# Tail values as 16 blocks in both attentions of a two-layer cross-attention kernel; other fillers, seeds, additions and mask conversions

## What is computed

```python
x = x + tanh(g_xattn[0]) * L0_xattn(layernorm(x), ctx_1024)            # no mask
x = x + tanh(g_ffn[0])   * L0_ffn(layernorm(x))                        # 512 -> 2048 relu -> 512
x = x + tanh(g_xattn[1]) * L1_xattn(ctx_1024, layernorm(x), mask)      # q, k, v normalised, masked
x = x + tanh(g_ffn[1])   * L1_ffn(layernorm(x))                        # fixed-point gelu
# attention: scores = q.k / sqrt(32); softmax over 154 keys; probs @ v; heads joined; @ W + b
```

## Time and profile before

| | |
|---|---|
| median of 3 executions | 2407.02 us (2404.2 to 2410.87) |
| the profiled execution | 2409.38 us, its span 2407.6 us |
| mean granted TensorE clock | 0.991 |
| VectorE, ScalarE, GpSimd busy | 1504.9, 1181.1, 238.6 us |
| memory traffic | read 105.30 MB, written 33.55 MB |

### The profile page before, as it was taken

One profiled execution on the slowest core, in us unless ns is written; L12 is line 12 of the kernel. 1 busy time (PEld: TensorE's weight loads), 2 busy tenths in 40 slices (PEclk: granted clock), 3 DMA queues, 4 the chain that ended last, 5 costly groups with the idle time before them and its releaser, 6 DMA issues.

```text
span 2407.6 us, 32695 instructions
## 1 busy us (share of the span) xinstructions
PE 2352.2 (98%) x12984; PEld 1793.4 (74%) x12984; DVE 1504.9 (63%) x2467; ACT 1181.1 (49%) x1912; POOL 238.6 (10%) x219
## 2 busy tenths in 40 slices
PE   7999999999999999999988999999999999999998
PEld 5566666688888888888765666666788888888886
DVE  5566666442222222223488888886988987988986
ACT  4554434442222222223335666666666666666665
POOL 1021112210000000000111111113000000000000
PEclk9999999999999999999998999999999999999999
DMA  3121112421101101102311111224301001110000
GB/s 130 36 88 53 53 54 80 161 80 53 50 4 53 53 1 53 53 3 86 121 64 50 67 68 67 67 71 145 105 29 43 36 36 36 36 38 33 36 35 19
DMA packets 89159, 140.95 MB, mean 59 GB/s; under 512 B 5040, under 2 KB 27952, under 8 KB 89008
## 3 DMA queue, kind: packets, MB, share of 16 engines
q1 hardware_dynamic: 89008, 138.87, 16.9%
HBM read 105.30 MB, written 33.55 MB: 58 GB/s over the span
## 4 chain that ended last, share of the span: by engine, by line
PE 39%; DVE 8%; ACT 2%; issue 2%; POOL 0%; DVEq 0%; ACTq 0%
PE l_lay_bank L69 19%; PE l_lay_score L69 11%; PE l_lay_score L1490 1%; PE l_lay_score L1546 1%; PE l_lay_score L1563 1%; DVE l_at_at_next L1089 1%; PE l_lay_score L1575 1%; PE l_lay_score L1567 1%; DVE l_at_h_lo L1103 1%; DVE l_at_at_next L1082 1%; PE l_lay_bank L1406 1%; DVE l_at_full L1078 1%; DVE l_at_full L1071 1%; DVE l_at_xTf_lo L975 1%; DVE l_at_maxes L1012 1%
## 5 line engine op out<-in xcount | busy, mean ns | idle before, releaser
L69 PE MATMUL l_lay_score<-l_at_tw_hi,l_at_h_hi 128*128 128x512 f32 x1024 | 401.5, 392 | 5.4 <-DVE l_at_h_lo L1103 4.8
L69 PE MATMUL l_lay_bank<-l_at_xTf_hi,l_at_tw_hi 128*128 128x512 f32 x1024 | 400.0, 391 | 0.0
L69 PE MATMUL l_lay_score<-l_at_tw_hi,l_at_h_lo 128*128 128x512 f32 x1024 | 398.8, 389 | 0.0
L69 PE MATMUL l_lay_bank<-l_at_xTf_hi,l_at_tw_lo 128*128 128x512 f32 x1024 | 398.4, 389 | 0.0
L69 PE MATMUL l_lay_bank<-l_at_xTf_lo,l_at_tw_hi 128*128 128x512 f32 x1024 | 398.4, 389 | 0.0
L69 PE MATMUL l_lay_score<-l_at_tw_lo,l_at_h_hi 128*128 128x512 f32 x1024 | 398.4, 389 | 0.0
L1063 DVE TENSOR_TENSOR l_at_h_lo<-l_at_full,l_at_h_hi 128x512 fp32r<-128x512 f32 x128 | 93.4, 729 | 468.5 <-ACT l_at_h_hi L760 468.5
L755 ACT ACTIVATE l_at_full<-l_lay_bank,l_at_lay_b 128x512 f32<-128x512 f32 x128 | 88.5, 691 | 456.6 <-PE l_lay_bank L69 456.6
L69 PEld LDWEIGHTS l_lay_score<-l_at_tw_hi,l_at_h_hi 128*128 128x128 f32 x1024 | 192.2, 188 | 49.3 <-DVE l_at_h_lo L1103 10.4
L69 PEld LDWEIGHTS l_lay_score<-l_at_tw_hi,l_at_h_lo 128*128 128x128 f32 x1024 | 192.2, 188 | 40.3
L69 PEld LDWEIGHTS l_lay_bank<-l_at_xTf_hi,l_at_tw_hi 128*128 128x128 f32 x1024 | 192.3, 188 | 40.1 <-issue 0.7
(11 more groups left out here) (196 smaller groups left out, 4063.0 us busy)
## 6 DMA issues: line engine op xcount, KB each, us to landing
both_x_in<-stream SPq DMA_DIRECT2D x25, 1024.0 KB, 5.6
l_at_xg<-stream SPq DMA_DIRECT2D x23, 1024.0 KB, 5.5
stream<-l_at_xg SPq DMA_DIRECT2D x22, 1024.0 KB, 4.3
l_at_tw_raw<-in_l_w SPq DMA_DIRECT2D x64, 256.0 KB, 5.5
both_x_in<-in_x SPq DMA_DIRECT2D x9, 1024.0 KB, 7.8
l_at_xg<-in_x SPq DMA_DIRECT2D x7, 1024.0 KB, 5.5
out<-l_at_xg SPq DMA_DIRECT2D x7, 1024.0 KB, 4.3
l_at_maskT_in<-in_maskT SPq DMA_DIRECT2D x16, 256.0 KB, 3.5
```

The source lines that it names most:

```text
L69: done = nc.tensor.matmul(out, lhs[a], rhs[b], start=first and n == 0, stop=last and n == len(passes) - 1)
```

## The change

Tail values of all four groups are made at once, in `tail_values` on TensorE: sixteen 32x32 blocks, group 0 into `values`, groups 1 to 3 into the score banks 1 to 3, where the tail scores have been read. VectorE copies group 1's to `c_sb`, ScalarE those of groups 2 and 3 (`tail_values_out`). The main values then start an accumulation of their own except in group 0. ScalarE's `c_evict` remains for group 0 only; for groups 1 to 3 VectorE adds the bank to `c_sb` (`c_add`), and `c_out` counts that. `tail_values` comes after the first q quarter (plain) or its first half (masked).

Plain layer: a q quarter stands between scores t-1 and t for every t, instead of two between values 0 and scores 2; two of the low parts and one `c_add` go between the first maxima.

Masked layer: q quarters 0 and 1 are cut in halves around `tail_values` and scores 0; each of the first two reciprocal transposes goes ahead of scores 1 and values 0; seeds are two by VectorE and two by ScalarE for each group; `mask_front` goes between VectorE's first two seeds, `maskT_front` to before the seeds of group 1, `norm_apply` to before q row 3. The output projection waits for low parts one by one.

```diff
@@ -701,9 +702,12 @@
                 act.wait_ge(maskT_done, 2 * it + 2)
-                act.wait_ge(exp_done, NS * it + GH * t + GH)
-                nc.scalar.activation(score[:, GH - 1, :], mask_main[:, it % 2, :], ACT.Copy)\
-                    .then_inc(act_seeded, 1)
+                for j in (2, 3):
+                    act.wait_ge(exp_done, NS * it + GH * t + j + 1)
+                    if t == 0:
+                        act.wait_ge(tail_v_act, 2 * it + j - 1)
+                    nc.scalar.activation(score[:, j, :], mask_main[:, it % 2, :], ACT.Copy)\
+                        .then_inc(act_seeded, 1)
 
@@ -719,6 +723,12 @@
                         .then_inc(exp_done, 1)
+
+            def tail_values_out(it, t):
+                act.wait_ge(tail_v_ps, 3 * it + t)
+                if it >= 2:
+                    act.wait_ge(cT_lo, KT * (it - 2) + t + 1)
+                nc.scalar.activation(c_sb[:, it % 2, t, :], score[:, t, :], ACT.Copy).then_inc(tail_v_act, 1)
 
@@ -821,33 +831,37 @@
                 exps_tail(it)
-                if norm:
-                    seed_main(it, 0)
                 if it < B:
                     v_tail_of(it)
-                if not norm:
+                if norm:
+                    tail_values_out(it, 2)
+                    tail_values_out(it, 3)
+                    seed_main(it, 0)
+                else:
                     if more:
...
                         relu_hi(0)
-                exps_main(it, 0)
-                if norm:
-                    seed_main(it, 1)
-                if not norm:
+                    tail_values_out(it, 2)
+                    tail_values_out(it, 3)
                     if more:
...
                         relu_hi(1)
+                exps_main(it, 0)
+                if norm:
+                    seed_main(it, 1)
+                if more and not norm:
+                    q_front(it + 1, (2,))
                 exps_main(it, 1)
...
                 c_evict(it, 0)
+                exps_main(it, 2)
                 if more and not norm:
-                    q_front(it + 1, (2, 3))
-                exps_main(it, 2)
+                    q_front(it + 1, (3,))
                 if norm:
                     seed_main(it, 3)
-                c_evict(it, 1)
                 if it and norm:
@@ -855,14 +869,12 @@
                     front.round_hi(act, "wd")
-                c_evict(it, 2)
                 if more and norm:
...
                     q_front(it + 1, (1,))
-                c_evict(it, 3)
                 if more and norm:
@@ -957,15 +969,20 @@
                     if it >= 2 and i:
-                        dve.wait_ge(act_seeded, KT * (it - 1))
-                        dve.wait_ge(dve_seeded, 3 * KT * (it - 1))
+                        dve.wait_ge(act_seeded, 2 * KT * (it - 1))
+                        dve.wait_ge(dve_seeded, 2 * KT * (it - 1))
                     nc.vector.tensor_scalar(to, maskT_in[:, i, :], 0, -BIG, ALU.is_equal,
...
                 dve.wait_ge(maskT_done, 2 * it + 2)
-                for j in range(GH - 1):
+                for j in range(2):
                     dve.wait_ge(exp_done, NS * it + GH * t + j + 1)
+                    if t == 0 and j == 1:
+                        if it < last:
+                            mask_front(it + 1)
+                        tail_values_out(it, 1)
+                        dve.wait_ge(tail_v_dve, it + 1)
                     nc.vector.tensor_copy(score[:, j, :], mask_main[:, it % 2, :]).then_inc(dve_seeded, 1)
@@ -1011,10 +1028,26 @@
 
+            def tail_values_out(it, t):
+                dve.wait_ge(tail_v_ps, 3 * it + t)
+                if it >= 2:
+                    dve.wait_ge(cT_lo, KT * (it - 2) + t + 1)
+                nc.vector.tensor_copy(c_sb[:, it % 2, t, :], score[:, t, :]).then_inc(tail_v_dve, 1)
+
+            def c_add(it, t):
+                c = c_sb[:, it % 2, t, :]
+                if t == 1:
+                    dve.wait_ge(tail_v_dve, it + 1)
+                else:
+                    dve.wait_ge(tail_v_act, 2 * it + t - 1)
+                dve.wait_ge(c_ps, KT * it + t + 1)
+                nc.vector.tensor_tensor(c, values, c, ALU.add).then_inc(c_out, 1)
+
             def c_back(it, ts):
...
                     c = c_sb[:, it % 2, t, :]
+                    dve.wait_ge(c_out, u + 1)
                     dve.wait_ge(rT_ps, u + 1)
@@ -1233,38 +1267,48 @@
                     q_rows_front(it + 1, (0,))
+                    maskT_front(it + 1)
                     seed_main(it, 1)
                     q_rows_front(it + 1, (1,))
-                    mask_front(it + 1)
-                    maskT_front(it + 1)
                     if it:
...
                     norm_stats(it + 2)
-                    q_rows_front(it + 1, (2, 3))
+                    q_rows_front(it + 1, (2,))
+                    norm_apply(it + 2)
+                    q_rows_front(it + 1, (3,))
                     q_norm_stats(it + 1)
                     seed_main(it, 3)
+                    c_add(it, 1)
                     q_norm_apply(it + 1)
                 else:
+                    tail_values_out(it, 1)
                     q_low(it + 1, (0, 1))
                     norm_stats(it + 2)
-                    q_low(it + 1, (2, 3))
+                    q_low(it + 1, (2,))
                     norm_apply(it + 2)
+                    q_low(it + 1, (3,))
+                    c_add(it, 1)
                 if it and norm:
...
                 elif it:
-                    c_back(it - 1, (0, 1))
-                if norm:
-                    norm_apply(it + 2)
+                    c_mult(it - 1, (0, 1))
+                c_add(it, 2)
                 if it and norm:
...
                 elif it:
-                    c_back(it - 1, (2, 3))
+                    c_mult(it - 1, (2, 3))
+                    c_low(it - 1, (0, 1))
                 if norm:
+                    c_add(it, 3)
                     q_low(it + 1, (0, 1))
...
                     max_of(it + 1, m)
+                    if m < 2 and it and not norm:
+                        c_low(it - 1, (m + 2,))
+                    if m == 2 and not norm:
+                        c_add(it, 3)
                     if m in (6, 9) and norm:
@@ -1537,18 +1590,39 @@
                         if i == 0:
-                            if not norm:
+                            if not norm and t == 0 and j == 1:
+                                pe.wait_ge(tail_v_dve, it + 1)
+                            elif not norm and t == 0 and j > 1:
+                                pe.wait_ge(tail_v_act, 2 * it + j - 1)
+                            elif not norm:
                                 pe.wait_ge(exp_done, NS * it + GH * t + j + 1)
-                            elif j < GH - 1:
-                                pe.wait_ge(dve_seeded, 3 * (KT * it + t) + j + 1)
                             else:
-                                pe.wait_ge(act_seeded, KT * it + t + 1)
+                                pe.wait_ge(dve_seeded if j < 2 else act_seeded,
+                                           2 * (KT * it + t) + j % 2 + 1)
                         nc.tensor.matmul(score[:, j, :], k2[a][rows[j], b, t, 0:P], q2[c][rows[j], t, :],
...
 
+            def tail_values(it):
+                b = it // CPB
+                pe.wait_ge(exp_done, NS * it + KT)
+                if it:
+                    pe.wait_ge(c_out, KT * it)
+                else:
+                    pe.wait_ge(kv_bias, 8)
+                if it % CPB == 0:
+                    pe.wait_ge(v_placed, V_COPIES * (b + 1))
+                for t in range(KT):
+                    for j in range(GH):
+                        c = own_rows[group_of(t, j)]
+                        to = score[own_rows[j], t, :] if t else values[own_rows[j], :]
+                        done = nc.tensor.matmul(to, keys.v_tail[c, b, t, own_rows[j]], p_tail[c, t, :],
+                                                start=True, stop=t > 0, skip_group_check=True)
+                    if t:
+                        done.then_inc(tail_v_ps, 1)
+
             def values_of(it, t):
@@ -1556,17 +1630,11 @@
                     pe.wait_ge(kv_bias, 8)
-                if t == 0 and it % CPB == 0:
-                    pe.wait_ge(v_placed, V_COPIES * (b + 1))
-                for j in range(GH):
-                    own = slice(DH * j, DH * (j + 1))
-                    nc.tensor.matmul(values[own, :], keys.v_tail[:, b, t, own], p_tail[:, t, :],
-                                     start=True, stop=False, skip_group_check=True)
                 for j in range(GH):
...
                                             keys.v_main[:, b, DH * head:DH * (head + 1)],
-                                            p_main[:, t % 2, j, :], start=False, stop=True,
+                                            p_main[:, t % 2, j, :], start=t > 0, stop=True,
                                             skip_group_check=True)
@@ -1613,8 +1681,10 @@
```

(31 more changed lines are left out.)

24 lines of the change are left out of this document (18 added, 6 removed).

## The result

| | before | after |
|---|---|---|
| median of 6 executions of each | 2406.88 us | 2422.33 us (2420.97 to 2431.23) |
| ratio, after to before | | 1.0071, 95% interval 1.0057 to 1.0084 |
| the profiled execution, its span | 2409.38, 2407.6 us | 2430.67, 2428.9 us |
| mean granted TensorE clock | 0.991 | 0.986 |

The change makes the kernel 15.4 us slower.

What follows compares the result with a forecast made beforehand. TensorE was taken to set the pace, with VectorE and ScalarE only just ahead of it. Plain layer -4.7 and masked layer +18.8 sum to +14.1 us on a median of 2407.02: forecast 2421, range 2392 to 2431.

Steps and rivals of the forecast that it cites:

- the collision: Masked chunks 2, 3, 4, 6: key-mask conversions meet GpSimd's residual addition, +2.6 waiting and +1.6 half clock, 4.9 us with common cost.
- Rival B: Waits on max 2 and scores 1 mostly absent, TensorE's saving reaches the end: 2372 in full, 2390 for half; chance 0.20.
- TensorE's saving: Tail values as one block of 1.07 us instead of 3.52, with 0.22 for shape changes: net 2.2 us per chunk.
- Rival D: The tail blocks do not run side by side: +2.4 us per chunk, partly inside waits, 2440; chance 0.03.
- Plain chunks 1 to 6: Plain layer: late maxima give back 1.4 of 2.2 us, leaving -0.8 per chunk, -4.7 for six.
- Chunk 0: Plain layer's first chunk, its maximum stage bound by VectorE: a gain of only 0.7 us.
- Plain chunk 7: Last plain chunk: no filler between scores 0 and scores 1, a wait of some 2.4 us, net +0.7.
- rival C: Every wait over 1 us also halves the clock, in masked waits and both last chunks: up to +8, 2430; chance 0.07.
- A common masked chunk: Masked layer: waits at scores 1 (+1.15), scores 3 (+0.35) and up to max 2 (+0.55) outweigh the saving: +0.7 us per chunk.
- The norm: Masked layer: applying the norm ahead of q row 3 moves 1.8 us of work and costs nothing, else under 1 us a chunk.
- Rival A: The meeting of conversions and residual addition is missed, four masked chunks fall from 4.9 to 0.7 us: 2404; chance 0.25.
- Masked chunk 7: Last chunk of the masked layer, without fillers: +0.9 us.

Runs made afterwards that it cites:

- e8: Changed kernel with residual addition later, three seeds by VectorE, new VectorE orders in both layers, last chunks' second product as filler again: 2389.52 us, 0.9920 of before.
- e1: Changed kernel, but in the masked layer GpSimd widens all four reciprocals before adding the bias to the residual: 2413.06 us, ratio to before 1.0017.
- e2: Changed kernel with the key-mask conversions put back behind q row 1, residual addition left in place: 2412.11 us, ratio to before 1.0018.
- e6: Changed plain layer with the old masked layer, VectorE's low parts spread between maxima and group 3's addition after maximum 6: 2406.35 us, ratio to before 0.9987.
- e7: Changed kernel, residual addition later except in the last chunk, VectorE's additions and low parts reordered in the masked layer: 2405.56 us, ratio to before 0.9983.
- e9: The changed kernel itself run once more, giving the second trace (profiled execution 2424.66 us): median 2421.76 us, ratio to before 1.0052.
- e3: Changed kernel, residual addition later except in the last chunk, seeds three by VectorE and one by ScalarE: 2406.23 us, ratio to before 0.9992.
- e4: Plain layer of the changed kernel with the masked layer of the kernel before: 2407.85 us, ratio to before 0.9997.
- e10: As e3, but the norm of x is applied at its old place, ahead of the low parts of groups 2 and 3: 2412.79 us, ratio to before 1.0018.
- e5: Masked layer of the changed kernel with the plain layer of the kernel before: 2433.53 us, ratio to before 1.0104.

## Why the prediction was right, and where not

The median is 2422 where 2421 was said, and the largest term, the collision, is what the runs show. That the total is right to about one us is luck. In the second trace, which is 15.3 us above that of before, the masked layer costs 14.4 where 18.8 was said, mainly because three chunks met and not four, and the plain layer with the turn costs 0.9 where a gain of 4.7 was said. The two errors cancel. (The range, too, starts at 2392, while the half case of B, which it is said to take in, is 2390.) In the order of the prediction:

**TensorE's saving.** The block takes 1.07 us, to the hundredth what the tail scores' rows gave. Rival D is out. Whether the net of 2.2 us a chunk is right could be read directly only where nothing is late, and no run has that; chunk 7 below gives an estimate of 2.4. The best case seen, e8, has plain chunks of 49.77 us, with 0.6 us of lateness still in them, against 51.02 before.

**Plain chunks 1 to 6.** The mechanism and its place were right: 0.51 us at max 2 (0.5 said), then steps longer than the usual 1.09 and 0.98 by 0.21, 0.43, 0.23 and 0.10 (0.2, 0.33, 0.33 said). Three steps late were priced and four were: -0.6 in four chunks instead of -0.8, while the first of the six gained 0.2 and the last nothing. Chunk 0 gained 1.5 where 0.7 was said. Chunks 0 to 6 gave 3.9 us, 5.4 were expected.

**Plain chunk 7.** The step that failed. I priced a wait of 2.4, set it against the saving and wrote +0.7. Up to the output projection (414.60 to 446.67 against 418.41 to 447.61) it cost 2.9. The wait itself was priced well: scores 1 stand still for 1.12 us, and then their first four matmuls start one by one behind the exponentials, 1.38 us up to the next four instead of 0.33, together 2.2. What was put at nothing is what comes behind it. The wait brought the clock down, which the forecast kept for rival C alone: from the second four of scores 1 to the last eight of the sums TensorE needs 4.44 us (430.28 to 434.72), where the kernel before needs 2.52 without its tail values, 1.9 more. Scores 3 take 0.4 more, and values 3 come 0.7 late behind the addition of group 2, which is behind two products and two low parts here too. These sum to 5.3, and 5.3 - 2.9 leaves 2.4 for the saving. TensorE's groups (scores 1, values 0), and the granted clock of 429 to 434, which is 0.66:

```profile
428.90 2.13 PE L1602 MATMUL l_lay_score<-l_at_qT_hi,l_at_k_hi 32*128 32x512 f32 x4 [1.12 <-ACT l_at_p_main L724]
...
432.25 1.79 PE L1635 MATMUL l_lay_score<-l_at_p_main,l_at_v_main 128*32 128x512 f32 x8
```

```profile
429.00:434.00 5.00, 5.00 (x28) 2.09 (x32) 1.59 (x1) 3.23 (x7) 5.00 (x2) 0.66 0.02 3
```

The remaining 1.4 us lie in the turn between the layers (from the last reciprocals to the second layer's start 776.4 before, 777.8 after). The traces with the new plain layer come in two kinds: after, e1, e2, e6, e7 and e9 have 48.4 us up to the last reciprocals and then 777.8 to 778.0, while e3, e4 and e10 have 49.96 and then 775.2. Chunk 7 and the turn together take 825.2 to 826.4 in all nine, and 822.0 in both traces with the old plain layer, so the change costs 3 to 4 us there in either kind. What makes the two kinds stays open.

**A common masked chunk.** +0.7 was said; 55.66 - 54.8 = +0.9 in e1. Scores 1 wait, spread over their first four matmuls, with ScalarE's seeds of 1.14 us behind its exponentials. In chunk 2 of the first trace they take 2.38 us to the transposes behind them, where scores 0 take 1.13, so they wait 1.25:

```profile
1373.30 1.75 PE L1602 MATMUL l_lay_score<-l_at_qT_hi,l_at_k_hi 32*128 32x512 f32 x4
...
1375.68 0.65 PE L1677 MATMUL l_lay_bank<-ident,l_at_r_wide 128*128 128x128 f32 x4
```

The prediction said 1.15; its own terms, 4.42 - 3.2, give 1.2, as 4.4 - 3.99 give 0.4 for scores 3 and not 0.35 (0.38 in the trace, 1.51 against 1.13). From the q transposes to max 2 it is 6.54 us in e1 (1439.48 to 1446.02) against 6.0 before, +0.54 against +0.55 said. Within it lie two waits, values 3 behind the addition of group 2 (0.62) and max 2 (0.80), and the prediction had put the first inside the second's path, which e3 and e7 bear out: in e3 the one grew as the other went, and in e7 both went, worth 1.47 together.

**The norm.** Laid at nothing. The new place costs little, 0.2 us a chunk in e3 (with three seeds by VectorE; in the changed kernel it was not isolated), and the sum needed only that. But the old place was no longer free: it costs 1.28, and e10, with the norm there, is 1.06 us a chunk slower, 6.6 us in all by the medians. As a part of its own the move is a gain, which the prediction missed for having asked only what the new place costs.

**The collision.** Right in place and mechanism, and nearly in price; wrong in which chunks meet. The count gave 5.7 us from the q product's start to the conversion and 5.6 to the addition; the trace has 1426.02 - 1420.17 = 5.85 and 5.86. The price is 3.84 us on top of a common chunk, 2.2 of waiting and 1.6 of half clock, where 2.6 + 1.6 = 4.2 was said. Rival A, missed collision, is out for chunks 3, 4 and 6 and right for chunk 2, where the residual landed at 12.1 us into the chunk (1371.24 - 1359.14), against less than 11.25 in chunk 3. Chunk 5 escaped, as said, for -0.4 (-0.5 said). Chunk 1 escaped in the second trace, for -4.8 (-3.2 said), and in the first it did not, for +2.1. That a chunk's outcome can change between executions was not in the prediction at all. Chunk 1 alone makes 6.9 us between the two traces, whose spans are 6.0 apart. The two levels of the first six executions are 9 apart, and the rest of that stays open. It is also the likely reason why the half change e5 lies above the whole.

The Trainium skill (SBUF — State Buffer, SBUF: two separate sides) speaks of an exclusive lock of a shared port, with the loser blocked; the rows of 4.79 and 3.36 us agree.

**Masked chunk 7.** +0.9 said, +2.8 measured: the wait of scores 1 (1.04, then four matmuls one by one, 2.07 from first start to last end instead of 0.51, and a granted clock of 0.50 from 1666 to 1669) and the one of values 3 (0.71), as in the plain layer. Both last chunks together were underpriced by about 4 us (2.2 and 1.9).

**The sum,** for the first trace: -3.9 + 4.3 for the plain layer with the turn (-4.7 said), and +1.7, +2.1, +0.7, +4.7, +4.6, -0.4, +4.7, +2.8 for masked chunks 0 to 7, 20.9 (18.8 said). Chunk 1 missed by 5.3 in one direction and chunk 2 by 4.2 in the other; both last chunks and the turn were under, which in the second trace the escaping chunk 1 gives back.

Rival B is out for the change as it stands: scores 1 and max 2 do wait. e8 shows how much of the saving could be had, some 19 us under before by the ratio and by the spans, once GpSimd's addition, VectorE's order and the fillers of the last chunks are put right. Rival C was right in the last chunks and nowhere else: the wait of 1.25 us ahead of scores 1 in chunk 2 did not lower the clock (values 0 behind it take 1.06 us, as always). Why the clock stayed there and fell behind the 1.12 and 1.04 of the last chunks stays open.

## What to carry to other kernels

Ask of a moved step not only what it costs at its new place but what its old place would cost after the rest of the change. Before putting a conversion within SBUF, or an operation on two SBUF operands, ahead of something TensorE waits for, look at what GpSimd does in that microsecond; if the two arrive within 0.1 us, plan for both outcomes, and expect a kernel whose time jumps between executions. Price the last chunk by itself: its fillers are gone and every wait there is bare.
